# The second attention of a fused kernel, with its score matrix laid out the other way round

## The reference

```python
def _L1_attn_ref(x, Wq, bq, Wk, bk, Wv, bv):
    q = x @ Wq + bq
    k = x @ Wk + bk
    v = x @ Wv + bv
    scores = jnp.einsum('btd,bsd->bts', q, k)
    attn = jax.nn.softmax(scores, axis=-1)
    return jnp.einsum('bts,bsd->btd', attn, v)
...
t = t + _L1_attn_ref(_ln_t(t), ...)
```

## Time and profile before

| what | value |
|---|---|
| median of 3 runs | 3510.87 us (3508.09 to 3511.03) |
| the profiled execution, its own time | 3511.96 us |
| its span, first to last instruction | 3510.2 us |
| busy share: PE, PEld, DVE, ACT, POOL | 97%, 75%, 75%, 57%, 47% |
| the second attention's first scores (L1264) | 2575.4 us |
| its last exponential (L1140) | 3339.0 us |

### The profile page before, as it was taken

How to read it: one execution, slowest core, us unless ns; L and a number is a source line. 1 busy time by engine, 2 the same in 40 slices (tenths; PEclk the granted TensorE clock), 3 DMA queues, 4 the chain that set the end, 5 groups by cost and what they waited for, 6 DMA issues and landing times. The chain is left out here.

```text
span 3510.2 us, 94134 instructions
## 1 busy us (share of the span) xinstructions
PE 3403.2 (97%) x30646; PEld 2643.6 (75%) x30646; DVE 2635.0 (75%) x6494; ACT 2015.6 (57%) x3642; POOL 1645.1 (47%) x863
## 2 busy tenths in 40 slices
PE   8799999999999999999999999999799999999978
PEld 5477777777777777777777777777578888888867
DVE  8688888888888888888888888888666675654457
ACT  4466666666666666666666666666435454455533
POOL 5566656556556556656656655655400001005112
PEclk9899999999999999999999999999899999999989
DMA  7642242234224224222422422222331020100011
GB/s 266 194 133 94 72 135 94 72 106 123 73 99 129 72 92 136 73 92 100 109 92 94 115 92 94 81 91 94 106 99 58 15 85 4 39 1 1 1 44 42
DMA packets 111794, 308.21 MB, mean 88 GB/s; under 512 B 11592, under 2 KB 72955, under 8 KB 91163
## 3 DMA queue, kind: packets, MB, share of 16 engines
q1 hardware_dynamic: 110629, 306.27, 27.9%
q10 hardware_dynamic: 1054, 0.48, 0.1%
HBM read 252.38 MB, written 54.31 MB: 87 GB/s over the span
## 5 line engine op out<-in xcount | busy, mean ns | idle before, releaser
L730 ACT ACTIVATE c_PT<-c_Tps 128x512 f32<-128x512 f32 x2592 | 1428.3, 604 | 877.8 <-PE c_Tps L860 815.7
L795 DVE CUSTOM_DVE_ANT_0 c_S<-c_Sps,mask_tiles 128x768 f32<-128x768 f32 x1728 | 1619.3, 956 | 412.6 <-PE c_Sps L849 371.8
L698 POOL TENSOR_SCALAR c_S<-c_S,c_row_max 128x2304 f32<-128x2304 f32 x576 | 1414.0, 2455 | 950.6 <-DVE c_row_max L806 950.6
L860 PE MATMUL c_Tps<-ident,c_S 128*128 128x128 f32 x10368 | 1400.8, 273 | 4.1 <-ACT c_PT L730 4.1
L860 PEld LDWEIGHTS c_Tps<-ident,c_S 128*128 128x128 f32 x10368 | 1229.7, 140 | 152.1 <-ACT c_PT L730 9.7
L849 PE MATMUL c_Sps<-c_K,c_Q 96*128 (+1 forms) x3456 | 854.6, 328 | 29.0 <-DVE c_part_max L795 14.6
L873 PE MATMUL c_Ops<-c_PT,c_V 128*32 128x256 f32 x10368 | 619.2, 382 | 0.8 <-ACT c_PT L730 0.8
L873 PEld LDWEIGHTS c_Ops<-c_PT,c_V 128*32 128x32 f32 x10368 | 307.4, 109 | 243.6 <-issue 51.1
L849 PEld LDWEIGHTS c_Sps<-c_K,c_Q 96*128 96x128 bf16 x3456 | 315.2, 98 | 188.4 <-issue 144.1
L1463 DVE TENSOR_SCALAR_CACHE_REDUCE l_S<-l_Sps,l_v 128x384 f32<-128x384 f32 x432 | 259.8, 618 | 252.9 <-PE l_Sps L1264 249.3
L1148 ACT ACTIVATE ln2T<-l_Tps 128x384 f32<-128x384 f32 x432 | 196.5, 491 | 363.6 <-PE l_Tps L1287 363.6
(11 more groups left out here) (223 smaller groups left out, 1644.2 us busy)
## 6 DMA issues: line engine op xcount, KB each, us to landing
mask_tiles<-in_mask SPq DMA_DIRECT2D x144, 1152.0 KB, 7.7
numerators<-c_O SPq DMA_DIRECT2D x288, 64.0 KB
mask_tiles<-numerators SPq DMA_DIRECT2D x7, 2304.0 KB, 8.5
q_parts<-c_PT SPq DMA_DIRECT2D x12, 576.0 KB, 4.4
k_parts<-c_PT SPq DMA_DIRECT2D x12, 576.0 KB
c_Q<-q_parts SPq DMA_DIRECT2D x71, 96.0 KB
c_vpad<-v_padded SPq DMA_DIRECT2D x8, 756.0 KB, 14.8
c_K<-k_parts SPq DMA_DIRECT2D x7, 864.0 KB, 8.6
```

The costliest lines, as they stand in the source:

```text
L698: pool.tensor_scalar(S[:, slot, :], S[:, slot, :], -1.0, row_max[:, slot:slot + 1], ALU.mult, ALU.add).then_inc(shifted, 1)
L730: act.activation(dst, src, ACT.Exp, scale=-1.0).then_inc(exp_done, 1)
L795: dve.tensor_tensor_reduce(out=S[:, r % ROW_SLOTS, cols(CH, c)].rearrange("p (k n) -> p k n", k=2), in0=Sps[:, n % S_SLOTS, :, 0:GW], in1= ...
L860: last = pe.transpose(Tps[:, g % T_SLOTS, cols(P, k)], S[:, (2 * b + t) % ROW_SLOTS, cols(P, kt)], ident[:, :])
```

## The change

The scores are computed with the keys on partitions. `scores` holds 128 keys as weights and streams 128 queries, 18 products for a tile, three to a PSUM bank, and ScalarE copies the banks to one of three buffers (`keys_by`), which need no transposes before the product with `v`. A query's maximum now lies across partitions. VectorE first takes the maximum over the 18 key blocks for every partition and query, in two halves that read the buffer with a step of 128 elements (`half_maximum`), and joins them (`key_maximum`). TensorE turns that 128 x 128 block (`turn_max`), VectorE reduces it to one maximum for each query and spreads it over 128 columns (`query_maximum`), TensorE turns it back (`spread_max`), ScalarE copies it to `shift` (`take_shift`), and it is subtracted from the scores: key blocks 0 to 8 by VectorE, 9 to 17 by GpSimd, both named `subtract_max`. Two exponentials of 1152 a row follow. The sum of the exponentials comes from a column of ones in `v`, as column 129 of the product. Scores run two tiles ahead (`AHEAD`). GpSimd's bias is issued a group at a time, and in the last image its `normal` steps two at a time behind a subtraction.

```diff
+        P_SLOTS = 3
+        keys_by = [slot.rearrange("p (t q) -> p t q", t=TILES) for slot in (S[:, 0, :], S[:, 1, :], ln2T[:, 3, :])]
+        half_max = sb("half_max", [P, 2, P])
+        key_max = sb("key_max", [P, 2, P])
+        query_max = sb("query_max", [P, 1])
+        max_wide = sb("max_wide", [P, P])
+        shift = sb("shift", [P, 1, P])
...
-        Sps = ps("Sps", [P, 3, BANK])
-        Tps = ps("Tps", [P, 3, BANK])
+        Tps = ps("Tps", [P, 4, BANK])
+        Mps = ps("Mps", [P, 2, BANK])
...
+            def subtract_max(j):
+                pool.wait_ge(shift_in, j + 1)
+                part = keys_by[j % P_SLOTS][:, HALVES[1].start:HALVES[1].stop, :]
+                pool.tensor_tensor(part, part, shift[:, :, :].to_broadcast([P, len(HALVES[1]), P]), ALU.subtract).then_inc(shifted_pool, 1)
...
+            bias(0, range(NG))
+            subtract_max(0)
+            normals = 0
+            for j in range(ALL):
+                b, qt = j // TILES, j % TILES
...
                         normal(n)
...
+                        normals = n + 1
...
+            def take_scores(j, chunks):
+                for g in chunks:
+                    if g == 0 and j >= P_SLOTS:
+                        act.wait_ge(o_ready, o_at(j - P_SLOTS) + 1)
+                    act.wait_ge(t_ready, scores_at(j) + g + 1)
+                    act.activation(keys_by[j % P_SLOTS][:, cols(GB, g), :],
+                                   Tps[:, (scores_at(j) + g) % T_SLOTS, 0:GW].rearrange("p (t q) -> p t q", t=GB), ACT.Copy).then_inc(t_taken, 1)
+            def take_shift(j):
+                act.wait_ge(shift_ready, j + 1)
+                act.activation(shift[:, 0, :], Mps[:, 1, 0:P], ACT.Copy).then_inc(shift_in, 1)
+            def exponentials(j, half):
+                act.wait_ge(shifted_pool if half else shifted_dve, j + 1)
+                part = keys_by[j % P_SLOTS][:, HALVES[half].start:HALVES[half].stop, :]
+                act.activation(part, part, ACT.Exp).then_inc(p_ready, 1)
...
+                    take_transposes(t_at(j), b + 1)
+                elif qt == TO_Q:
+                    take_queries(t_at(j), b + 1)
+                if j + AHEAD < ALL:
+                    take_scores(j + AHEAD, range(4))
+                if j + 1 < ALL:
+                    take_shift(j + 1)
+                if j + AHEAD < ALL:
+                    take_scores(j + AHEAD, range(4, NG))
+                if j + 1 < ALL:
+                    for half in range(2):
+                        exponentials(j + 1, half)
...
+            def scores(j, chunks):
+                b, qt = j // TILES, j % TILES
+                n = scores_at(j)
+                if qt == 0:
+                    pe.wait_ge(t_taken, (t_at(TILES * (b - 1) + TO_Q + 1) if b else T_PREP) + T_SLOTS)
+                query_tile = qT[:, bass.ds((b % 2) * N + qt * P, P)]
+                for g in chunks:
                     pe.wait_ge(t_taken, n + g + 1)
                     for k in range(GB):
...
+                        last = pe.matmul(Tps[:, (n + g) % T_SLOTS, cols(P, k)], lnT[:, bass.ds((b % 2) * N + (g * GB + k) * P, P)], query_tile,
+                                         start=True, stop=True)
+                    last.then_inc(t_ready, 1)
+            def turn_max(j):
+                pe.wait_ge(key_max_ready, j + 1)
+                pe.transpose(Mps[:, 0, 0:P], key_max[:, j % 2, :], ident[:, :]).then_inc(turned_max, 1)
+            def spread_max(j):
+                pe.wait_ge(wide_max, j + 1)
+                if j:
+                    pe.wait_ge(shift_in, j)
+                pe.transpose(Mps[:, 1, 0:P], max_wide[:, :], ident[:, :]).then_inc(shift_ready, 1)
+            def values(j, half):
+                b, qt = j // TILES, j % TILES
+                if half == 0:
+                    pe.wait_ge(o_taken, o_at(j) + 1)
+                pe.wait_ge(p_ready, 2 * j + half + 1)
+                for kt in HALVES[half]:
...
+                    project(b + 1, o_at(j, after=False))
+                elif qt == TRANSPOSE:
+                    transpose_ln(b + 1, t_at(j))
+                elif qt == TO_Q:
+                    to_q(b + 1, t_at(j))
+                elif qt == TO_V:
+                    to_v(b + 1, o_at(j, after=False))
+                if j + AHEAD < ALL:
+                    scores(j + AHEAD, range(4))
+                    spread_max(j + 1)
+                    scores(j + AHEAD, range(4, NG))
+                values(j, 0)
+                if j + AHEAD == ALL:
+                    spread_max(j + 1)
+                values(j, 1)
+                if j + AHEAD < ALL:
+                    turn_max(j + AHEAD)
...
+            def half_maximum(j, half):
+                dve.wait_ge(t_taken, scores_at(j) + NG * (half + 1) // 2 + T_SLOTS)
+                part = keys_by[j % P_SLOTS][:, HALVES[half].start:HALVES[half].stop, :].rearrange("p t q -> p q t")
+                dve.tensor_reduce(half_max[:, half, :], part, AX.X, ALU.max).then_inc(half_step, 1)
+            def key_maximum(j):
+                dve.wait_ge(half_step, 2 * (j + 1))
+                dve.tensor_tensor(key_max[:, j % 2, :], half_max[:, 0, :], half_max[:, 1, :], ALU.max).then_inc(key_max_ready, 1)
+            def query_maximum(j):
+                b, qt = j // TILES, j % TILES
+                dve.wait_ge(turned_max, j + 1)
+                dve.tensor_reduce(query_max[:, :], Mps[:, 0, 0:P], AX.X, ALU.max).then_inc(query_step, 1)
+                dve.wait_ge(query_step, j + 1)
+                if j:
+                    dve.wait_ge(shift_ready, j)
+                if qt == 0:
+                    dve.wait_ge(o_taken, (o_at(TILES * (b - 1) + TO_V) if b else O_PREP) + O_SLOTS)
+                constant = v[:, (b % 2) * TILES + qt, 0:1]
+                dve.scalar_tensor_tensor(out=max_wide[:, :], in0=query_max[:, :].to_broadcast([P, P]), scalar=constant,
+                                         in1=constant.to_broadcast([P, P]), op0=ALU.add, op1=ALU.subtract).then_inc(wide_max, 1)
+            def subtract_max(j):
+                dve.wait_ge(shift_in, j + 1)
+                part = keys_by[j % P_SLOTS][:, HALVES[0].start:HALVES[0].stop, :]
+                dve.tensor_tensor(part, part, shift[:, :, :].to_broadcast([P, len(HALVES[0]), P]), ALU.subtract).then_inc(shifted_dve, 1)
+            def take_row(j):
+                b, qt = j // TILES, j % TILES
+                dve.wait_ge(o_ready, o_at(j) + 1)
+                dve.reciprocal(inv_total[:, qt % 2:qt % 2 + 1], Ops[:, qt % 2, C:C + 1]).then_inc(inv_step, 1)
+                dve.wait_ge(inv_step, j + 1)
+                dve.scalar_tensor_tensor(out=row(b, qt), in0=Ops[:, qt % 2, 0:C], scalar=inv_total[:, qt % 2:qt % 2 + 1], in1=row(b, qt),
                                          op0=ALU.mult, op1=ALU.add).then_inc(o_taken, 1)
...
+            for j in range(ALL):
+                b, qt = j // TILES, j % TILES
+                if j:
+                    take_row(j - 1)
+                if b + 1 < B and qt == PROJECT:
+                    take_projected(b + 1, o_at(j, after=False))
+                if b + 1 < B and qt == TO_V:
+                    take_v(b + 1, o_at(j, after=False))
+                if j and j + 1 < ALL:
+                    query_maximum(j + 1)
+                if j:
+                    row_statistics(j - 1)
+                if j + AHEAD < ALL:
+                    half_maximum(j + AHEAD, 0)
+                if j + 1 < ALL:
+                    subtract_max(j + 1)
+                if j + AHEAD < ALL:
+                    half_maximum(j + AHEAD, 1)
+                    key_maximum(j + AHEAD)
+                if b + 1 < B:
+                    if qt == 0:
+                        invert(b + 1)
...
```

More of the change, by code:

```diff
@@ L1130, in take_normal @@
                     act.wait_ge(t_ready, n + g + 1)
[L1131 removed]
+                    act.activation(ln2T[:, b, cols(GW, g)], Tps[:, (n + g) % T_SLOTS, 0:GW], ACT.Copy,
                                    accum_out=sums[:, b, g:g + 1]).then_inc(t_taken, 1)
[L1134 to L1149 removed]
@@ L1324, in _ @@
-            for qt in range(TILES):
-                if qt in TO_EXPERTS:
-                    transpose_normal(TO_EXPERTS.index(qt), t_at(B - 1, qt, last=True, after=False))
-                following = (B - 1, qt + 1, (qt + 1) % 2) if qt + 1 < TILES else None
-                if following is not None:
-                    scores(*following, groups=FIRST)
-                attend(B - 1, qt, qt % 2, last=True, last_scores=following)
+            scores(0, range(NG))
+            scores(1, range(3))
@@ L1563, in last_tile @@
-            def last_tile(qt, t, ahead=2, values=True):
-                if ahead:
-                    take_scores(B - 1, qt + 1, 1 - t, t_at(B - 1, qt, True))
-                if ahead > 1:
-                    stage(B - 1, qt + 2, t)
-                invert_total(B - 1, qt, t)
-                if values:
-                    take_values(B - 1, qt - 1, 1 - t, last=True)
```

(38 more changed lines are left out.)

308 lines of the change are left out of this document (101 added, 207 removed).

## The result

The changed kernel takes 3557.84 us (median of 4 runs, 3555.52 to 3559.87), the kernel before 3509.70 beside it (4 runs, 3508.09 to 3511.03). The ratio is 1.0137, with a 95% interval of 1.0123 to 1.015: slower by 48 us. The profiled execution has a span of 3555.0 us, 44.8 more than before.

What follows compares the result with a forecast made beforehand. TensorE bounds the old kernel (9.86 us a tile), VectorE's loop the new (9.65). On 3511.96 us, -14.5 + 8 + 41 + 9 + 5 gives 3560.5, 3559 at the median; range 3450 to 3605, the forecast's own 3530 to 3590.

Steps and rivals of the forecast that it cites:

- plain tiles: 69 periods of the tile loop at 9.65 us in place of 9.86: -14.5 us.
- the preparation with its clock: Next image's preparation on VectorE stalls TensorE, +41 us for three images; lowered clock behind the longest stall, +9.
- start, end and last image: Unfilled first and last tiles, +8 us; GpSimd's `normal` steps holding `key_maximum` in the last image, +5.
- The loop: Waits from one tile's first score product through VectorE's maxima and subtraction to `turn_max`: a period of 9.65 us.
- the strided reduction: VectorE's `half_maximum`, reading with a step of 128 elements: 1.94 us, the middle of 1.34 and 2.54.
- the estimate by a page: `half_maximum` at the skill's 1.73 ns a column: 2.14 us, period 9.85, total about 3575 us.
- GpSimd's subtraction: GpSimd's half of the subtraction, 1152 columns, on the line through 384 and 768: 2.30 us, ending at 6.0.
- The blocking: VectorE's and GpSimd's subtractions don't overlap; the second waits for the other's whole instruction, costing 1.25 us a tile.
- Rival 3: VectorE's and GpSimd's subtractions overlap, period 8.4 us: 3463 us, or 3431 with the dense reduction rate; chance 0.20.
- Rivals 1: VectorE's strided reduction runs at the dense rate, with the blocking as forecast: 3516 us; chance 0.17.
- 2: VectorE's strided reduction costs double the dense time for each element: 3613 us; chance 0.13.
- rival 4: Bound doesn't move: VectorE's preparation fits into unseen waits and only the plain terms count: 3510 us; chance 0.05.

Runs made afterwards that it cites:

- experiment 1: The changed kernel with the two half-maximum reductions reading their 1152 elements densely instead of with a step of 128: 3505.89 us, ratio 0.999.
- experiment 9: The eighth kernel with GpSimd subtracting 12 of the 18 key tiles and VectorE 6, exponentials and values following: 3468.84 us, ratio 0.9886.
- experiment 12: The changed kernel with GpSimd subtracting its half of the scores from itself, not the repeated shift: 3522.23 us, ratio 1.0038.
- experiments 2: The changed kernel with GpSimd's subtraction cut to one element, so half the scores go unshifted: 3481.54 us, ratio 0.9921.
- 3: The changed kernel with both halves of the subtraction on VectorE, none on GpSimd: 3565.21 us, ratio 1.0156.
- 4: The changed kernel with both halves of the subtraction on GpSimd, none on VectorE: 3517.85 us, ratio 1.0024.
- the eighth kernel: The changed kernel with VectorE's subtraction after its maxima, halves exchanged, key maximum a one-input reduction, square roots ahead of exponentials: 3474.60 us, ratio 0.9907.

## Why the prediction was right

The mechanism was right: VectorE's blocked subtraction and its slow second reduction set the tile, and the preparation on VectorE stalls TensorE. That the total, 3559 for 3557.84, is within 1.2 us is luck. On the spans, the forecast of +48.5 was -14.5 for plain tiles, +50 for the preparation with its clock and +13 for start, end and last image; the measured +44.8 are +16.6, +31 and -3. The first was 31 us too low, even in its sign, and the other two together 35 too high.

**The loop.** From the first score product (3194.51) as time 0, forecast and measured: `spread_max` out 2.79 and 2.69, shift copy 3.3 and 3.28, GpSimd's start 3.7 and 3.63, its end 6.0 and 6.27, VectorE's subtraction done 7.25 and 7.48, second half maximum 9.15 and 9.56, key maximum 9.5 and 9.89, period 9.65 and 10.10. Every step was in its place. Two durations were short: GpSimd's 2.30, which was 2.64, and the strided reduction's 1.94, which was 2.16 to 2.18. So the plain term was +16.6 us and not -14.5.

**The strided reduction.** I took the middle of 1.34 and 2.54. The measured 2.18 (dense 1.34, experiment 1) is nearest to 2.14, the estimate by a page that I had set beside the sum: the Trainium skill (Vector Engine (DVE) Microarchitecture Reference, section 5.2) gives 1.73 ns a column for a source that hops at every element. The trace agrees with the estimate within 2%, though the page's hop is 4 KiB and this one 512 bytes.

**GpSimd's subtraction.** The line through its steps of 384 and 768 columns gave 2.30 at 1152. Measured were 2.64, and 3.465 at 1536 columns (experiment 9), 2.15 ns for each column between them. The Trainium skill (GPSIMD Engine Reference, section 3.1) has 4497 ns for a two-input step of 2048 float32 elements, 2.2 ns each. An estimate by it is 2.53 for 1152, nearer to 2.64 than my line; the 2.11 of experiment 12 is below both.

**The blocking** held in full: experiments 2, 3, 4 and 12 show it from four sides. The Trainium skill (GPSIMD Engine Reference, section 1, Specifications) says that GpSimd's SBUF interfaces are shared with VectorE, with contention where VectorE's instruction has two SBUF inputs or is in a two-port mode. The runs agree on the first, and give its price: the whole of the other's instruction. On the second they have only the copy of 2.48 us, and nothing here shows its mode. Rival 3, that the two subtractions overlap, is refuted, and with it went the chance of a faster kernel. Rivals 1 and 2 fell with the reduction's 2.18, rival 4 with the stalls.

**The preparation.** Forecast were 13.7 us an image and 3 for the clock, measured 9.3, 9.3 and 12.3 for both. The tiles with `sum_half` took 12.03 (1.9 over, forecast 2.3), those with `finish_half` 10.82 (0.7, forecast 1.0), the one after the statistics 11.56 (1.5, forecast 1.8). For `normalise` I had 5.1. It ran from the key maximum to its end in 6.6 us, close to the 6.9 forecast, and TensorE was idle for 2.41 ahead of its transposes, which then go at VectorE's pace:

```profile
2916.51 0.33 PE L1313 MATMUL l_Mps<-ident,l_key_max 128*128 128x128 f32 x1 [1.61 <-DVE l_key_max L1503]
2919.24 4.40 PE L1272 MATMUL l_Tps<-ident,ln2T 128*128 128x128 f32 x18 [2.41 <-DVE ln2T L1484]
```

The same 18 transposes in the kernel before, and the scores behind them:

```profile
2888.58 2.44 PE L1234 MATMUL l_Tps<-ident,ln2T 128*128 128x128 f32 x18
2890.86 3.39 PE L1264 MATMUL l_Sps<-l_lnT,l_q_tile 128*128 128x384 f32 x10
```

This tile took 16.90 us, 6.8 above a plain one, where the transposes had cost 2.28: 4.5 of stall. The stalls come to 11.4 us an image, each a little under its forecast. What brings them to 9.3 the forecast had left out: beside the preparation TensorE had lost some 2 us an image in the kernel before too (17.6, of which 15.7 are the four steps' own work). The third image's 3 us more, the held copy and the clock behind it, weren't in it either.

**The clock** did fall in this tile, to 0.52 in 2921 to 2923 (nearly all of it at the lower level, 1.2 GHz), after 0.33 us of work in the 3 us before 2919. There it cost nothing: from the first transpose to the next scores TensorE took 4.24 us (VectorE's normalisation 4.70), and 4.23 in the eighth kernel, where the clock stayed at 1.00. It had a price in two other places at least:

```profile
2594.00:2598.00 4.00, 4.00 (x25) 4.00 (x25) 3.72 (x10) 2.32 (x4) 0.67 (x1) 0.66 0.06 18
3091.00:3094.00 3.00, 3.00 (x17) 3.00 (x18) 0.89 (x3) 0.00 (x0) 0.00 (x0) 0.57 0.00 0
```

The first is the first full iteration: its 24 score records took 4.0 us for 2.7, and the tile 1.4 more. The second stands in the third image, behind 3.43 us without work: the products of `project` took 5.9 us for 4.7 in the other images.

**Start, end and last image**: forecast +13, measured -3. The first full iteration came 22.8 us in and not 26 (2571.22 to 2594.03), the first scores themselves were 4.2 us earlier than before, and plain tiles of the last image took the same 10.10 us, with a few at 10.23, so `normal` hardly held the key maximum.
